# Attention: weighted sums over two blocks of queries, with the row sums as a row of them

## The reference

```python
q, k, v = split_heads(x @ Wq.T + bq), split_heads(x @ Wk.T + bk), split_heads(x @ Wv.T + bv)   # 16 heads of 16
scores = q @ k.T / 4 + gate_out * pos_bias            # 8 x 16 x 1024 x 1024
attn = softmax(scores, axis=-1)
out = (attn @ v) -> (8, 1024, 256)
return out @ Wo.T + bo
```

## Time and profile before

| | |
|---|---|
| median of 3 runs | 4017.55 us (4009.93 to 4023.25) |
| profiled execution | 4000.15 us |
| its span in the trace | 3998.3 us |
| attention | from about 373 to 2533 us of the span |
| busy over the span: PE, DVE, ACT, POOL | 3523.8, 2410.7, 2381.2, 1221.6 us |
| mean granted TensorE clock | 0.956 of full |

### The profile page before, as it was taken

How to read it: one execution, slowest core, us unless ns; L and a number is a source line. 1 busy time by engine, 2 the same in 40 slices (tenths; PEclk the granted TensorE clock), 3 DMA queues, 4 the chain that set the end, 5 groups by cost and what they waited for, 6 DMA issues and landing times. The chain is left out here.

```text
span 3998.3 us, 97133 instructions
## 1 busy us (share of the span) xinstructions
PE 3523.8 (88%) x33340; PEld 2750.0 (69%) x33716; DVE 2410.7 (60%) x5410; ACT 2381.2 (60%) x4590; POOL 1221.6 (31%) x1533
## 2 busy tenths in 40 slices
PE   4994998998989989989999899785699999999993
PEld 2552776776767767767677677675588888888882
DVE  3664998898889988989889899576011111111115
ACT  2553998898989989989889899311222222222221
POOL 1332332332323323323233233037322222222221
PEclk9996999999999999999999999896799999999996
DMA  5667242242432332424232423564455555555556
GB/s 172 203 206 151 31 83 55 39 88 43 95 63 37 71 66 31 96 41 93 55 49 68 70 31 73 143 206 143 172 172 190 173 187 177 184 190 172 193 178 204
DMA packets 243211, 468.95 MB, mean 117 GB/s; under 512 B 35474, under 2 KB 138772, under 8 KB 224146
## 3 DMA queue, kind: packets, MB, share of 16 engines
q1 hardware_dynamic: 200466, 393.04, 37.1%
q0 software_dynamic: 26880, 35.87, 4.2%
q10 hardware_dynamic: 15360, 33.56, 2.4%
HBM read 309.87 MB, written 152.58 MB: 116 GB/s over the span
## 5 line engine op out<-in xcount | busy, mean ns | idle before, releaser
L660 DVE CUSTOM_DVE_ANT_0 sc<-sc,gbias 128x1024 f32<-128x1024 f32 x1024 | 1261.7, 1233 | 274.6 <-issue 198.9
L713 ACT ACTIVATE probs<-sc,negm 128x1024 f32<-128x1024 f32 x1024 | 1141.3, 1115 | 190.4 <-DVE negm L660 188.1
L569 POOL TENSOR_SCALAR gbias<-slab_a,gs 128x484 f32<-128x484 f32 x1024 | 683.8, 668 | 1487.6 <-DVE negm L660 1456.5
L602 PEld LDWEIGHTS pt<-ident,probs 128*128 128x128 f32 x8192 | 966.5, 142 | 203.2 <-issue 11.4
L602 PE MATMUL pt<-ident,probs 128*128 128x128 f32 x8192 | 1070.5, 274 | 1.4 <-issue 1.1
L724 ACT ACTIVATE pts<-pt 128x512 f32<-128x512 f32 x1280 | 733.6, 595 | 10.8 <-PE pt L602 10.6
L1211 ACT ACTIVATE f_hid<-f_ph,f_w_up 128x256 f32<-128x256 f32 x576 | 272.6, 473 | 719.0 <-PE f_ph L1172 719.0
L584 PE MATMUL sc<-ks,qs 128*128 128x512 bf16 x1672 | 542.2, 389 | 164.8 <-issue 68.7
L620 PE MATMUL pop<-pts,vs 128*32 128x128 f32 x16384 | 603.3, 277 | 18.0 <-DVE pts L670 6.3
L670 DVE COPY pts<-pt 128x512 f32<-128x512 f32 x768 | 525.5, 684 | 8.8 <-PE pt L602 8.8
L1172 PE MATMUL f_ph<-f_xt,f_w_up 128*128 128x256 f32 x2304 | 511.5, 380 | 2.6 <-DMA f_w_up<-in_w_up 1.9
(11 more groups left out here) (155 smaller groups left out, 2274.8 us busy)
## 6 DMA issues: line engine op xcount, KB each, us to landing
f_w_down<-in_w_down SPq DMA_DIRECT2D x72, 1152.0 KB, 5.3
f_w_up<-in_w_up SPq DMA_DIRECT2D x72, 1028.0 KB, 7.7
xg_d<-fill SPq DMA_DIRECT2D x16, 1820.0 KB, 16.5
ks<-k_d SPq DMA_DIRECT2D x192, 128.0 KB
qs<-q_d SPq DMA_DIRECT2D x192, 128.0 KB
f_xin<-xg_d SPq DMA_DIRECT2D x72, 260.0 KB, 5.2
v_d<-vt SPq DMA_DIRECT2D x16, 1024.0 KB, 6.5
vs<-v_d SPq DMA_DIRECT2D x32, 512.0 KB
```

The source lines that it names most:

```text
L569: pool.tensor_scalar(gbias[r % 4][:, SIDE:SIDE + BAND], slab[:, r % 4, :], gs[k % 2][:, r // 4, r % 4:r % 4 + 1], 1.0, ALU.mult, ALU.mult) ...
L602: mm = pe.transpose(pt[:, bank(k, r, half), j, :], probs[:, r % 2, jj * P:(jj + 1) * P], ident[:])
L660: dve.tensor_tensor_reduce(sc[:, r % 2, :], sc[:, r % 2, :], gbias[r % 4][:, w:w + N], -1.0, 3.0e38, ALU.add, ALU.min, negm[:, r % 4:r % 4 ...
L713: act.activation(probs[:, r % 2, :], sc[:, r % 2, :], ACT.Exp, bias=negm[:, r % 4:r % 4 + 1], scale=-1.0, accum_out=sums[:, i % 2, hh:hh + ...
```

## The change

The unit of the weighted sums becomes a pair of blocks, 256 queries. `pts` is twice as wide, and each weighing matmul has 256 moving columns. The four parts (two chunks each) of pair rows 0 to 7 lie in turns x = 8 to 11, `x % 8 < 4`. The row sums are no longer accumulated by the exponential: they are taken from row 16 of each head's sums. ScalarE copies `po` (128 x 256) to SBUF as `raw` in turn `x % 8 == 4`; TensorE multiplies it in turn `x % 8 == 5` by a constant `sum_row` that has ones where a head's 32 outputs meet its row 16, which gives the sums spread over 32 rows; VectorE takes in turn `x % 8 == 6` the reciprocal of all 128 x 256 and multiplies. Gone are the small reciprocal, its widening, the spreading transpose and the copy of its result.

```diff
+    c["c_sums"] = (np.arange(P)[:, None] == np.arange(P)[None, :] // 32 * 32 + D).astype(np.float32)
...
-        pts = sb("pts", [P, 2, 4, NI, P])
+        pts = sb("pts", [P, 2, 4, NI, 2 * P])
         negm = sb("negm", [P, 4])
-        sums = sb("sums", [P, 2, 4])
-        rsum = sb("rsum", [P, 2, 4])
-        rs = sb("rs", [P, 2, 4, 32])
-        rsb = sb("rsb", [P, P])
+        sum_row = sb("sum_row", [P, P])
+        raw = sb("raw", [P, 2 * P])
+        inv = sb("inv", [P, 2 * P])
...
-        po, pr = pop[:, 0, 0:P], pop[:, 1, 0:P]
+        po, pr = pop[:, 0, :], pop[:, 1, :]
...
-        def blocks_before(m, k, i):
-            return m * NI + (i - 1 if i > 0 or k > 0 else 0)
+        NP2 = NI // 2
+
+        def pairs_before(m, k, i):
+
+
+            return m * NP2 + (i // 2 - 1 if i > 1 or k > 0 else 0)
...
+            sp.dma_start(sum_row[:], a["c_sums"]).then_inc(sum_row_in, 16)
...
 
...
                         if part == 0:
-                            na, nv = halves(4 * i + 3, 1)
+                            na, nv = halves(4 * i + 7, 1)
                             pe.wait_ge(copied_a, m * SA + na)
                             pe.wait_ge(copied_v, m * SV + nv)
 
                             if i > 0:
-                                pe.wait_ge(ot_done[k % 2], uses(body, k) * NI + i)
+                                pe.wait_ge(ot_done[k % 2], uses(body, k) * NP2 + i // 2)
                             else:
-                                pe.wait_ge(ot_done[(k + 1) % 2], uses(body, k + 1) * NI)
-                        for j in range(3 * part, min(3 * part + 3, NI)):
+                                pe.wait_ge(ot_done[(k + 1) % 2], uses(body, k + 1) * NP2)
+                        for j in (2 * part, 2 * part + 1):
                             for hh in range(4):
-                                mm = pe.matmul(po[32 * hh:32 * hh + 32], vs[k % 2][:, j, 32 * hh:32 * hh + 32], pts[:, i % 2, hh, j, :],
+                                mm = pe.matmul(po[32 * hh:32 * hh + 32], vs[k % 2][:, j, 32 * hh:32 * hh + 32], pts[:, i // 2 % 2, hh, j, :],
                                                start=j == 0, stop=j == NI - 1, skip_group_check=True)
-                        if part == 2:
-
-                            pe.wait_ge(rs_done, m * NI + i + 1)
-                            pe.transpose(pr, rs[:, i % 2, :, :].rearrange("p h o -> p (h o)"), ident[:]).then_inc(av_done, 1)
+                        if part == 3:
+                            mm.then_inc(av_done, 1)
+
+                    def spread_sums(k, i):
+                        m = body * STEPS + k
+                        pe.wait_ge(raw_done, m * NP2 + i // 2 + 1)
+                        pe.matmul(pr, sum_row[:], raw[:], start=True, stop=True).then_inc(sums_done, 1)
...
-                    for x in range(len(rows) + 4):
+                    for x in range(len(rows) + 6):
                         if x < len(rows):
                             pe.wait_ge(exp_done, (body * STEPS + rows[x][0]) * R + rows[x][1] + 1)
                             if x + 2 < len(rows):
                                 scores(*rows[x + 2])
                             turn(*rows[x])
-                        if x >= 4:
-                            k, r = rows[x - 4]
-                            if r % 4 < 3:
-                                weigh(k, r // 4, r % 4)
+                        if x >= 8:
+                            k, r = rows[(x - 8) // 8 * 8]
+                            if x % 8 < 4:
+                                weigh(k, r // 4, x % 8)
+                            elif x % 8 == 5:
+                                spread_sums(k, r // 4)
...
-                            if hh == 1:
-                                dve.wait_ge(av_done, blocks_before(m, k, i))
-                            dve.tensor_copy(pts[:, i % 2, hh, 4:8, :], pt[:, bank(k, r, 1)]).then_inc(copied_v, 1)
-
-                    def reciprocals(k, i):
-                        m = body * STEPS + k
-                        dve.wait_ge(exp_done, m * R + 4 * i + 4)
-                        dve.reciprocal(rsum[:, i % 2, :], sums[:, i % 2, :]).then_inc(recip_done, 1)
-                        dve.wait_ge(recip_done, m * NI + i + 1)
-                        dve.wait_ge(av_done, blocks_before(m, k, i))
-                        dve.tensor_copy(rs[:, i % 2], rsum[:, i % 2, :].rearrange("p (h o) -> p h o", o=1).to_broadcast([P, 4, 32])).then_inc(rs_done, 1)
+                            if hh == 1 and i % 2 == 0:
+                                dve.wait_ge(av_done, pairs_before(m, k, i))
+                            dve.tensor_copy(pts[:, i // 2 % 2, hh, 4:8, i % 2 * P:(i % 2 + 1) * P], pt[:, bank(k, r, 1)]).then_inc(copied_v, 1)
 
                     def finish(k, i):
                         m = body * STEPS + k
+                        dve.wait_ge(sums_done, m * NP2 + i // 2 + 1)
+                        dve.sem_inc(sums_seen, 1)
+                        dve.reciprocal(inv[:], pr).then_inc(inv_done, 1)
                         if i == 0:
                             dve.wait_ge(ot_stored[k % 2], uses(body, k) * 16)
-                        dve.wait_ge(rcopied, m * NI + i + 1)
-                        dve.wait_ge(av_done, m * NI + i + 1)
-                        dve.tensor_tensor(ot[:, k % 2, i * P:(i + 1) * P], po, rsb[:], ALU.mult).then_inc(ot_done[k % 2], 1)
-
-                    for x in range(len(rows) + 6):
+                        dve.wait_ge(inv_done, m * NP2 + i // 2 + 1)
+                        dve.sem_inc(sums_seen, 1)
+                        dve.tensor_tensor(ot[:, k % 2, i * P:(i + 2) * P], raw[:], inv[:], ALU.mult).then_inc(ot_done[k % 2], 1)
+
+                    for x in range(len(rows) + 7):
                         if x < len(rows):
                             bias_and_max(*rows[x])
-                        if x >= 6 and rows[x - 6][1] % 4 == 3:
-                            finish(rows[x - 6][0], rows[x - 6][1] // 4)
+                        if x >= 14 and x % 8 == 6:
+                            finish(rows[(x - 14) // 8 * 8][0], rows[(x - 14) // 8 * 8][1] // 4)
                         if 2 <= x <= len(rows) + 1:
-                            k, r = rows[x - 2]
-                            copy_out(k, r)
-                            if r % 4 == 3:
-                                reciprocals(k, r // 4)
+                            copy_out(*rows[x - 2])
 
...
-                        if hh == 0:
-                            act.wait_ge(rs_done, blocks_before(m, k, i))
-                        act.activation(probs[:, r % 2, :], sc[:, r % 2, :], ACT.Exp, bias=negm[:, r % 4:r % 4 + 1], scale=-1.0,
-                                       accum_out=sums[:, i % 2, hh:hh + 1]).then_inc(exp_done, 1)
+                        act.activation(probs[:, r % 2, :], sc[:, r % 2, :], ACT.Exp, bias=negm[:, r % 4:r % 4 + 1], scale=-1.0).then_inc(exp_done, 1)
...
-                                if hh == 0 and half == 0:
-                                    act.wait_ge(av_done, blocks_before(m, k, i))
-                                act.activation(pts[:, i % 2, hh, 4 * half:4 * half + 4, :], pt[:, bank(k, r, half)], ACT.Copy).then_inc(copied_a, 1)
-
-                    def copy_sums(k, i):
+                                if hh == 0 and half == 0 and i % 2 == 0:
+                                    act.wait_ge(av_done, pairs_before(m, k, i))
+                                act.activation(pts[:, i // 2 % 2, hh, 4 * half:4 * half + 4, i % 2 * P:(i % 2 + 1) * P], pt[:, bank(k, r, half)], ACT.Copy).then_inc(copied_a, 1)
+
+                    def copy_raw(k, i):
                         m = body * STEPS + k
-                        act.wait_ge(av_done, m * NI + i + 1)
-                        act.activation(rsb[:], pr, ACT.Copy).then_inc(rcopied, 1)
+                        act.wait_ge(av_done, m * NP2 + i // 2 + 1)
+                        act.wait_ge(inv_done, m * NP2 + i // 2)
+                        act.wait_ge(ot_done[k % 2], uses(body, k) * NP2 + i // 2)
+                        act.wait_ge(ot_done[(k + 1) % 2], uses(body, k + 1) * NP2)
+                        act.activation(raw[:], po, ACT.Copy).then_inc(raw_done, 1)
...
-                    for x in range(len(rows) + 5):
-                        if x > R and x % R == 10:
+                    for x in range(len(rows) + 6):
+                        if x > R and x % R == 16:
                             store(x // R - 1)
                         if x < len(rows):
                             exponential(*rows[x])
-                        if x >= 5 and rows[x - 5][1] % 4 == 3:
-                            copy_sums(rows[x - 5][0], rows[x - 5][1] // 4)
+                        if x >= 12 and x % 8 == 4:
+                            copy_raw(rows[(x - 12) // 8 * 8][0], rows[(x - 12) // 8 * 8][1] // 4)
                         if 1 <= x <= len(rows):
                             copy_out(*rows[x - 1])
```

(30 more changed lines are left out.)

## The result

The changed kernel takes **4749.81 us** (median of 4 runs, 4738.26 to 4767.47), the one before 4013.74 on the same chip: a ratio of **1.183** [1.179, 1.188], 736 us slower. The forecast was 4594 in a range of 4420 to 4760. The runs of this study lie on several chips, on which the kernel before takes 4014 to 4096 us. So kernels are compared by their ratio to the kernel before on the same chip; 0.01 of it is 40 us, and 0.3 us in each of the 120 finishes that stall.

What follows compares the result with a forecast made beforehand. TensorE was taken as the bound, chained closely with VectorE and ScalarE. Pairs of 20.8 us against 16.18, plus start, end and drain, gave 72.1 us more per body, +577 over 8 bodies: 4594 us, range 4420 to 4760.

Steps and rivals of the forecast that it cites:

- row 7: Turn 7 of a pair's eight rows; TensorE was to have nothing for 3.6 us ahead of it.
- its own unknown costs: Reciprocal -30 to +50, links of the walk +-0.3 us (+-36): together 4530 to 4660.
- The bound and the bursts: TensorE's weighing is bound by columns; only the 0.16 us fixed price per burst goes, 0.3 us per pair.
- The reciprocal: VectorE's reciprocal of 128x256 in the finish was to cost 1.85 us, bounds 1.6 to 2.3.
- cheap reciprocal: Rival: the reciprocal costs 0.43, the stall is 1.4 us shorter on 120 finishes, -170, 4424; chance 0.15.
- The walk: One pair followed across the engines from TensorE's row 4: period 20.8 us against 16.18, 4.6 more per pair.
- row 4: Walk's zero, where TensorE begins this row of a pair; ScalarE copies the raw sums here, waiting for the last part.
- TensorE's row 5: Walk step: exponential 5 reaches TensorE at 2.18; its scores and transposes, 1.41, precede the spread.
- The clock: Rival: clock falls behind TensorE's idle 3.6 us per pair, +2 us, +240, 4834; chance 0.16, half for only some pairs.
- The forecast's likeliest case: Queues stall each pair at the finish, 20.8 us per pair, 4594 us; chance 0.61.
- Faster: the sums decide: Rival: reciprocal fits VectorE's slack, TensorE never runs dry, period 15.8, 3968; chance 0.06.
- Its point of decision: That rival wins if the wait at finish is shorter than VectorE's lead, about one row (2 us).

Runs made afterwards that it cites:

- run 10: Pairs and 256-column weighing with the row sums of the kernel before, weighing parts in turns 1, 3, 5, 7, later steps moved too: ratio 0.982 to the kernel before.
- run 1: Changed kernel plus 24 unused bf16 matmuls of 256 columns filling TensorE's gap in every turn x % 8 == 6: ratio 1.133 to the kernel before.
- run 3: Changed kernel with the reciprocal replaced by a copy and 12 unused matmuls filling TensorE's gap: ratio 1.091 to the kernel before.
- run 6: Changed kernel's instructions in other turns: weighing 1 to 4, raw-sums copy 6, spread 7, finish 1 of the next eight: ratio 1.070 to the kernel before.
- run 7: Changed kernel with its steps moved to roomier turns (finish in the next eight rows) and the reciprocal replaced by a copy: ratio 1.032.
- run 9: Pairs and 256-column weighing with the row sums of the kernel before, parts bunched in turns 0 to 3: ratio 1.024 to the kernel before.
- run 2: Changed kernel with the 128x256 reciprocal replaced by a copy, the division left out: ratio 1.122 to the kernel before.
- run 4: Changed kernel with only VectorE's finish moved one turn later, to x % 8 == 7: ratio 1.122 to the kernel before.
- run 5: The changed kernel itself measured again beside other runs: ratio 1.180 to the kernel before.

## Why the prediction was right, and where it fell short

Direction, cause and size came as forecast, in the main: the queues hold the kernel up at the finish, ahead of row 7, by the amount that was walked. That the time is within the range is partly luck. 4750 lies 10 us under the range's end, and above the 4530 to 4660 that the forecast gave for its own unknown costs. What carried it there is a fall of the clock that the forecast left out, and that stood among the rivals with 0.16.

**The bound and the bursts: right.** Wide matmuls brought nothing by their number: 565.5 us busy after, against 603.3 before with twice the records, and part of the 565.5 is at the lower clock. Only the bursts' fixed price is saved; I took it as 0.16 and it is 0.26. The missing 0.10 was in the 0.97 for eight transposes, read ahead of a burst and used for every row; without a burst behind it a row is 1.31, not 1.41 (run 10).

**The reciprocal: right.** 1.757 us measured, 1.85 forecast from three small sizes: 6.3 ns for each element beyond four. The rival "cheap reciprocal" falls. The estimate by the Trainium skill (VectorE: DVE Perf Modes, First, the fixed hardware budget), which reads its repeat count of 8 as 8 cycles an element, was 2.1 us; the measurement decides for less, about 6 cycles for each further element at that page's 0.96 GHz.

**The walk: right to 0.4 us.** From row 4's start, forecast and measured in the pair at 1306.44: TensorE's row 5 at 2.18, 2.07; reciprocal 4.38, 4.13; product 6.42, 6.02; maximum 7 at 6.76, 6.36; maximum 8 at 8.51, 8.11; exponential 8 at 9.92, 9.50. The gap was 3.6, and 3.41 came. A row's scores now come 1.18 us after the exponential's start (1307.33 to 1308.51), 1.17 forecast. Most of the 0.4 us is the reciprocal (1.76 for 1.85), the link from TensorE's row 5 to it (2.06 for 2.20), and the 0.19 us for the semaphore behind it, for which no row was shown; 0.13 lie there. With the clock held by filler matmuls the whole period was 20.5 against 20.8.

**The clock: the step that failed.** The forecast's likeliest case left the clock up, and gave its fall 0.16, because at 919.19 the matmuls still ran at full speed after 3.91 us of idle. That row was no evidence against a fall. The next instruction of the same trace, 4.8 us later, is at the lower level:

```profile
924.01 1.03 PE L584 MATMUL sc<-ks,qs 128*128 128x512 bf16 x2 [4.01 <-ACT probs L713]
```

The other row cited, 1193.71, stands in the same place, behind scores at full speed (1189.20) and a second gap. A body's start has two such gaps; behind the first the clock is up in three of the seven starts between bodies, behind the second it is down in all seven. In the changed kernel the gaps come every 20 us, and by the periods the clock was down behind them, for some rows at least, in 104 of 112 steady pairs; behind the gap shown at 1315.37 it was down from the first scores on. The rival's size was about right: 2 us per pair reckoned, 2.2 in the pair shown (22.69 less 20.47), 1.6 in the mean (22.0 less 20.43 of run 1). Its chance was far too low. The sum: 4594, less 0.4 x 120 = 48 for the links that I had too long, plus 190 to 200 for the clock by run 1, gives 4736 to 4746, against 4750 measured.

**The rivals.** "Faster: the sums decide" is refuted: TensorE's sum of under 16 us was never reached with this order. Its point of decision was the right one, VectorE's lead: it waits 2.06 us at the finish, a full row.

**How the 18% divide:** the clock 0.05 (run 1); the reciprocal's extra 1.33 us 0.04 (runs 1 and 3; again 6 and 7); the turns of the steps about 0.06 (run 1 to run 6, which moves all of them at once, and in which the clock nearly holds, too). What is left, 0.03, was not taken apart in this form of the kernel; bunched weighing, 0.024 in run 9, would be most of it, and the rest of the finish the remainder. How much of the 0.06 is ScalarE's wait in row 4 and how much VectorE's in row 6 was not tried apart.

## What to carry to other kernels

When engines are chained through two buffers, the turn of a step can matter more than its cost: here a step issued one turn after what it needs stopped its whole queue, and what stood behind it was what the critical engine needed. Before merging small matmuls into wide ones, divide a long burst's time by its columns; if it is at the columns' rate, only the bursts' fixed price can be saved, and the parts must stay spread over the rows. Moving a per-row scalar's work to a full tile, here two reciprocals of 4 columns to one of 256, multiplies the work of an operation whose price per element is nearly five times that of a copy (6.3 ns against 0.68 us for 512 elements). And a gap in TensorE costs twice where the clock falls behind it. The state of the clock is read behind every gap of a kind, not behind one.

## What was not expected of the hardware

A gap of 2.1 us on TensorE, between stretches in which it is nearly always busy, was enough to bring the clock to 1.2 GHz in the pair shown of run 2, and gaps of 0.96 and 1.34 us in run 4, while the kernel of run 6, whose gaps are under 1 us each in the steady part, keeps 0.98 of the clock over 300 us. The length of the gap alone doesn't decide. Behind equal gaps the clock fell in some pairs and not in others: 8 of 112 pairs of the changed kernel, with gaps of 3.4 us, show no loss, and 12 of 112 in run 5, the first twelve of the stage in a row; so do 23 of 112 in run 2, and 61 of 112 in run 4. What decides was not tried. Filling 2.6 of 3.4 us with useless matmuls kept it up and made the kernel 4% faster. Entering a burst of 32-column matmuls from 128-column transposes costs 0.10 us ahead of it, besides the 0.16 that the burst takes beyond its records.
